# A fused RWKV layer and quantised feed-forward: the first of three matrix powers takes 48 columns instead of 64, and four engines' orders are rewritten

## The reference, cut to what matters

```python
x = x + attn(layernorm(x)) ; x = x + int8_linear(layernorm(x))

# attn: token shift, low-rank mixing into four inputs, then
r, k, v = xrg @ Wr.T, xk @ Wk.T, xv @ Wv.T          # and gates a, ma, mk, decay w, output gate g
kk = normalised per head(k + tanh(xk @ kkk_w1.T) @ kkk_w2);  b = -kk * a
def step(s, (q, w, k, v, a=kk, b)):                  # one token, per head, s is 32x32
    sa = s @ a
    s  = s * w + outer(sa, b) + outer(v, k)
    return s, s @ q
y = groupnorm(y) * ln_w + ln_b + (r*k*faaaa).sum(per head) * v
return (y * g) @ Wo.T

# int8_linear: each row is quantised to int8 by its own maximum, multiplied, scaled, bias added
```

## Time and profile before

| | us |
|---|---|
| median of 3 runs | 3148.51 |
| lowest, highest | 3138.39, 3151.72 |
| the profiled execution's own time | 3128.81 |
| its span, first to last instruction | 3126.8 |

### The profile page before, as it was taken

The page is one execution under the profiler, slowest core; times in us unless marked ns, Lnnn a source line. Parts: engine busy times, 40 slices in busy tenths (PEclk is TensorE's granted clock), DMA queues, the critical chain, the costliest instruction groups (busy, mean ns, idle before and its releaser), DMA issues.

```text
span 3126.8 us, 176469 instructions
## 1 busy us (share of the span) xinstructions
PE 2899.6 (93%) x80128; PEld 2566.1 (82%) x80128; DVE 2496.5 (80%) x4803; ACT 1997.2 (64%) x4486; POOL 1456.9 (47%) x1224
## 2 busy tenths in 40 slices
PE   5999999999999999999999999999999999999995
PEld 5888888888888888888888888888888888888873
DVE  4787887878887888877788788888788887888875
ACT  4666666656666666656666666666666666666663
POOL 5445444445444454444444444544444544544542
PEclk9999999999999999999999999999999999999997
DMA  4122222222222222222222222222222222222211
GB/s 132 41 63 52 47 64 50 47 50 56 56 51 47 64 51 47 64 50 47 50 48 64 51 47 64 51 47 64 51 47 55 60 47 51 56 55 52 63 41 39
DMA packets 92610, 170.74 MB, mean 55 GB/s; under 512 B 13908, under 2 KB 14932, under 8 KB 91864
## 3 DMA queue, kind: packets, MB, share of 16 engines
q1 hardware_dynamic: 91864, 159.45, 21.6%
HBM read 41.97 MB, written 16.78 MB: 19 GB/s over the span
## 4 chain that ended last, share of the span: by engine, by line
PE 86%; issue 5%; DVE 5%; POOL 3%; ACT 1%; DVEq 0%; POOLq 0%; ACTq 0%
PE bank L1228 33%; PE bank_a L1367 12%; PE bank L1429 8%; PE bank_b L1398 4%; PE bank_b L1419 4%; PE bank_b L1345 4%; PE bank_a L1345 4%; PE bank L1235 4%; PE bank_b L1408 3%; PE bank L1310 2%; PE bank L1445 2%; POOL xm_wa L417 1%; PE bank_a L1383 1%; PE bank L1281 1%; PE bank_a L1375 1%
## 5 line engine op out<-in xcount | busy, mean ns | idle before, releaser
L537 ACT ACTIVATE bank<-bank,maa 128x128 f32<-128x128 f32 x1024 | 276.9, 385 | 103.2 <-PE bank L1281 103.2
L1006 DVE STREAM_TRANSPOSE stacked<-bank_b 32x256 f32<-32x256 f32 x512 | 229.2, 448 | 107.7 <-PE bank_b L1419 100.6
L1228 PE MATMUL bank<-xm_rg,w_r 128*128 128x128 f32 x2048 | 280.8, 285 | 7.6 <-issue 6.9
L1228 PE MATMUL bank<-xm_v,w_v 128*128 128x128 f32 x2048 | 281.8, 281 | 2.3 <-issue 2.1
L1429 PE MATMUL bank<-w_o,yc 128*128 128x512 f32 x512 | 259.2, 610 | 12.1 <-DVE yc L826 11.6
L1367 PE MATMUL bank_a<-pw,w_ffn_int 32*32 32x64 f32 x16384 | 258.7, 215 | 3.8 <-DVE pw L826 2.0
L1228 PEld LDWEIGHTS bank<-xm_rg,w_r 128*128 128x128 f32 x2048 | 243.7, 191 | 22.6 <-issue 8.4
L421 POOL TENSOR_TENSOR rs<-rs,minus_half 128x1 f32<-128x1 f32 x64 | 86.6, 1354 | 375.2 <-DVE rs L842 375.2
L1228 PEld LDWEIGHTS bank<-xm_v,w_v 128*128 128x128 f32 x2048 | 253.0, 194 | 8.5 <-issue 2.7
L1367 PEld LDWEIGHTS bank_a<-pw,w_ffn_int 32*32 32x32 f32 x16384 | 236.4, 105 | 23.9 <-issue 13.3
L1228 PEld LDWEIGHTS bank<-xm_k,w_k 128*128 128x128 f32 x2048 | 240.4, 193 | 10.8 <-issue 1.9
(11 more groups left out here) (188 smaller groups left out, 8127.5 us busy)
## 6 DMA issues: line engine op xcount, KB each, us to landing
streamed<-aq_state SPq DMA_DIRECT2D x128, 384.0 KB, 5.2
streamed<-w_ffn_int SPq DMA_DIRECT2D x128, 384.0 KB, 5.3
xin<-in_x SPq DMA_DIRECT2D x128, 128.0 KB, 5.0
xres<-in_x SPq DMA_DIRECT2D x128, 128.0 KB, 2.8
out<-o_sb SPq DMA_DIRECT2D x128, 128.0 KB
w_ffn_int<-in_weight_q SPq DMA_DIRECT2D x1, 2048.0 KB, 10.5
w_k<-in_Wk SPq DMA_DIRECT2D x1, 1024.0 KB
w_r<-in_Wr SPq DMA_DIRECT2D x1, 1024.0 KB
```

The source lines that it names most:

```text
L537: return nc.scalar.activation(out_, in_, func, **kw)
L1006: ins = V.transpose(to[:, :, 1 - c, :], step_part(NEW)[quad(h)])
L1228: ins = mm(bank[:, o * n:(o + 1) * n], weights[:, k, o * P:(o + 1) * P], x[:, k].rearrange("p b t -> p (b t)"), start=(k == 0), stop=(k == ...
```

## The change

The crossing block and the matrix are now neighbours: `first` becomes three sets of G groups with 2 parts each, laid out group by group, where it was six slabs. Set 0 holds the matrix and the crossing block of the tile in work; sets 1 and 2 are the score sets of odd and even tiles for `from_solutions`. The first power multiplies only the 48 columns that are not the identity. The identity's share of the sum, which is the matrix's own right half plus the halves' identity, is formed by two GpSimd sums straight into the right half of `pw`, and `power(m, 1)` on PE waits for them by the new semaphore `g_id`. DVE's sum after the first power then covers 16 columns per group instead of 32. No calls are added or dropped beside the two on POOL; the calls of `tile_step` are in a new order on POOL, ACT, DVE and PE. SP's order stays.

```diff
-        first = sb("first", [P, 6, G, CHUNK])
+        first = sb("first", [P, 3, G, 2, CHUNK])
...
+            def diagonal_sums(m):
+                pool.wait_ge(v_pm, count(m, 1, 1))
+                pool.wait_ge(p_t, count(m, 1, 0))
+                pool.wait_ge(a_tx, count(m, 1, 0))
+                pool.wait_ge(v_t4, count(m, 1, 0))
+                add(pw[:, :, 1, HALF:], first[:, 0, :, 0, 0:HALF], first[:, 0, :, 0, HALF:]).then_inc(g_id, 1)
+
+            def diagonal_ones(m):
+                pool.wait_ge(g_id, count(m, 2, 1))
+                add(pw[:, :, 1, HALF:], pw[:, :, 1, HALF:],
+                    ident_half[:].unsqueeze(1).to_broadcast([P, G, HALF])).then_inc(g_id, 1)
...
             def crossing(m):
                 act.wait_ge(v_pm, count(m, 1, 1))
                 act.wait_ge(v_sums, count(m, POWERS, 0))
-                run(first[:, 1, :, 0:HALF], pairs(bank_a)[:, :, 0, HALF:], ACT.Identity,
+                run(first[:, 0, :, 1, 0:HALF], pairs(bank_a)[:, :, 0, HALF:], ACT.Identity,
...
             def scores_b(m):
                 dve.wait_ge(p_sb, count(m, 1, 1))
-                own = 2 + 2 * (m % 2)
-                tt(first[:, 0:own + 1:own].rearrange("p j g t -> p g j t"), pairs(bank_a), mask_b[:].unsqueeze(1).to_broadcast([P, G, 2, CHUNK]),
+                dve.wait_ge(g_id, count(m, 2, 0))
+                own = 1 + m % 2
+                tt(first[:, 0:own + 1:own, :, 0, :].rearrange("p j g t -> p g j t"), pairs(bank_a), mask_b[:].unsqueeze(1).to_broadcast([P, G, 2, CHUNK]),
...
-                before = first[:, 1] if k == 0 else pw[:, :, 1, :]
-                tt(pw[:, :, 1, :], pairs(bank_a)[:, :, 1, :], before, ALU.add).then_inc(v_sums, 1)
+                if k == 0:
+                    tt(pw[:, :, 1, 0:HALF], pairs(bank_a)[:, :, 1, 0:HALF], first[:, 0, :, 1, 0:HALF],
+                       ALU.add).then_inc(v_sums, 1)
+                else:
+                    tt(pw[:, :, 1, :], pairs(bank_a)[:, :, 1, :], pw[:, :, 1, :], ALU.add).then_inc(v_sums, 1)
...
+                if k == 1:
+                    pe.wait_ge(g_id, count(m, 2, 2))
                 pe.wait_ge(v_ptT, count(m, POWERS + 1, k + 1))
                 for n, g, q in ALL:
-                    ins = mm(bank_a[q, 64 * n:64 * n + 64], pt[q, g, :],
-                             first[q, 0:2, g] if k == 0 else both(pw[q, g]), start=True, stop=True)
+                    if k == 0:
+                        ins = mm(bank_a[q, 64 * n:64 * n + 48], pt[q, g, :], both(first[q, 0, g])[:, 0:48],
+                                 start=True, stop=True)
+                    else:
+                        ins = mm(bank_a[q, 64 * n:64 * n + 64], pt[q, g, :], both(pw[q, g]), start=True, stop=True)
...
                 for j, g, q in step_pairs(c):
                     ins = mm(bank[q, 4 * CHUNK * j + CHUNK:4 * CHUNK * j + 3 * CHUNK], both(u2[q, j]),
-                             first[q, own:own + 2, g], start=False, stop=True,
+                             both(first[q, own, g]), start=False, stop=True,
```

More of the change, by code:

```diff
@@ L196, in rwkv_ffn_kernel @@
         a_pw, a_u, a_y, a_g, a_b2, a_k2, a_vT2 = (sem(f"a_{n}") for n in "pw u y g b2 k2 vT2".split())
-        g_qk, g_qkf, g_rkv, g_aqs = (sem(f"g_{n}") for n in "qk qkf rkv aqs".split())
+        g_qk, g_qkf, g_rkv, g_aqs, g_id = (sem(f"g_{n}") for n in "qk qkf rkv aqs id".split())
         a_e, a_tx, a_xm = sem("a_e"), sem("a_tx"), sem("a_xm")
@@ L494, in tile_step @@
                     norm_rstd(j)
+                if solve:
+                    bonus(m)
+                    diagonal_sums(m)
+                    diagonal_ones(m)
+                    weighted_bonus(m)
                 if project:
-                    kept_keys(i)
                     keys_undecayed(i)
@@ L500, in tile_step @@
                 if project:
+                    kept_keys(i)
+                    keys_weighted(i)
                     removals_undecayed(i)
-                    keys_weighted(i)
-                if solve:
-                    weighted_bonus(m)
                 if finish:
@@ L737, in tile_step @@
                     keys(i)
+                if solve:
+                    key_pairs(m)
+                if finish:
+                    solution(n, 1)
+                if project:
                     ma_gate(i)
                     a_gate(i)
-                if finish:
-                    solution(n, 1)
                 if solve:
+                    value_pairs(m)
                     crossing(m)
-                    key_pairs(m)
                 if project:
@@ L1104, in tile_step @@
                     update_state(n, 1)
-                if mix:
-                    norm_moments(j)
-                if project:
-                    removal_keys(i)
                 if solve:
                     removals_turned(m)
+                    bonus_rows(m)
+                if project:
+                    decay_sums(i)
                 if finish:
                     heads_turned(n)
-                if mix:
-                    norm_variance(j)
-                if project:
-                    decay_sums(i)
                 if solve:
@@ L1147, in tile_step @@
                     shift_mix(j)
-                if project:
-                    removal_directions(i)
                 if solve:
                     power(m, 2)
-                    bonus_rows(m)
+                if project:
+                    key_norm_spread(i)
+                    removal_directions(i)
+                    removals_decayed(i)
                 if finish:
```

104 lines of the change are left out of this document (49 added, 55 removed).

## The result

The changed kernel takes **3169.91 us** (median of 6 runs, 3161.45 to 3181.53) against 3144.18 us for the kernel before (6 runs, 3128.29 to 3151.72). The ratio is 1.010, 95% interval 1.007 to 1.013 (the two medians alone give 1.008): slower by about 1%, where 3120 us was forecast. The profiled execution took 3165.46 us.

The account below looks back on a forecast made before the run. PE was taken to set the pace, with waits for POOL and for late code. Minus 25.6, plus 9 and minus 12 made minus 28.6 us, 0.91% off 3148.5: 3120 us, 8-in-10 range 3092 to 3148.

Parts of the forecast that it names:

- The first power: PE's first power with 48 instead of 64 columns: 0.40 us less per tile, minus 25.6 us, bounds 0 and minus 45.
- The flat price of the first rival: First power: 48 columns cost about what 64 do, saving some 8 us in all; part of a rival with chance 0.22.
- Late code: Holes without a semaphore at the first power take back part of its gain: plus 9 us, bounds 0 and plus 12.
- the 35 us that I had named as a sign of being wrong: Holes at the first power of more than 35 us would show the prediction wrong.
- The wait for `xm_wa`: PE's wait for POOL at `hidden` gets shorter by 0.35 us in 35 tiles: minus 12 us, bounds 0 and minus 38.
- The wait for `g_id` and the two sums: At PE's second power: POOL's two sums end about 4 us before PE asks, so no cost.
- ACT's value copies ahead of `crossing`: ACT before the first power: four value copies, 2.66 us, stay hidden with 0.2 to 0.7 us to spare; zero.
- My slower side: Rival, chance 0.08: ACT's value copies end after PE is ready for the first power; 3184 us.
- `xn` ahead of the affine pieces: ACT before the output projection: spare time falls from 0.88 to 0.16 us; zero, upper bound plus 19 us.
- the term that I put at zero for everything else that moved: Other moved calls, on engines with idle time, end over half a us ahead of their readers; no cost.
- The clock: PE's mean clock was 0.968; a mean off by over 0.01 from that would show the prediction wrong.
- The rival of the eaten gain: Chance 0.22: 48 columns cost about what 64 do or late code takes the gain, and `xm_wa` is no sooner; 3141 us.

Follow-up runs that it names:

- pool_back: The changed kernel with GpSimd's kept_keys and keys_weighted back in their old places: 3099.21 us, ratio 0.9885 to the kernel before.
- act_back: The changed kernel with only ACT's normalised(j) back ahead of power(m, 1): 3122.02 us, ratio 0.996 to the kernel before.
- columns_only: The kernel before with the 48 columns, the new layout and the two sums, all its orders kept: 3132.43 us, ratio 0.9985.
- pool_back_64: The changed kernel with GpSimd's kept_keys and keys_weighted in their old places and 64 columns in the first power: 3107.13 us, ratio 0.9882.
- pool_back_32: The changed kernel, GpSimd's kept_keys and keys_weighted in old places, 32 columns in the first power, crossing-block product left out: 3112.76 us, ratio 0.9882.

## Why the prediction was wrong

*The first power, minus 25.6:* right. The batch is busy 1.56 us; in all 107.8 us against 133.8, minus 26.0. The flat price of the first rival doesn't hold for this packing: 1.56 us lies between the 1.29 us with 32 columns and the 1.99 with 64.

*Late code, plus 9:* near in size at its place (25.9 to 37.2 us, plus 11.3, and past the 35 us that I had named as a sign of being wrong), too small as a whole. All of PE's waits without a semaphore went from 128.0 to 160.0 us, plus 32, where my bound was 12. `solve_step` (L1428) gained 13.6 us of them and `inverse` (L1403) 4.1, which I had not asked about. The hole that the earlier trace rows show behind 122 records is there again, in the same place, with 48 columns:

```profile
1521.48 1.54 PE L1385 MATMUL bank_a<-first,w_ffn_int 32*32 32x48 f32 x122
1525.27 0.28 PE L1385 MATMUL bank_a<-first,w_ffn_int 32*32 32x48 f32 x6 [2.25 <-issue]
```

*The wait for `xm_wa`, minus 12:* right, 38.0 to 25.2 us, minus 12.8.

*The wait for `g_id` and the two sums, 0:* right. They take 0.73 us each, and PE never waits for them; the old code without them is no faster.

*ACT's value copies ahead of `crossing`, 0:* right. PE waits 0.6 us for `first` in the whole run. My slower side was this one, and it didn't happen.

*`xn` ahead of the affine pieces, 0 with 0.16 us to spare:* right by itself. In a tile of `pool_back` the gate product ends at 1548.59 and `project_out` starts at 1548.78, 0.19 to spare. But `act_back` shows what giving up 0.7 us of room meant: it bounds what any later delay may be, and I went on to price the others as if the room were still there.

*The step that failed* is the term that I put at zero for everything else that moved, in the sentence that "all else that moved (`bonus_rows`, `decay_sums`, `kept_keys`, `finish_rows`) lies on engines with idle time and ends ahead of its reader by over half a us". DVE never waited for `kept`, so its reader did have it in time. What it delayed is an operation of another engine that neither reads it nor is read by it: the gate product, 1.71 us instead of 0.69, and with it `project_out`. An idle engine isn't free to be used where its work shuts out a busy one. The price, from `after` to `pool_back`: 1.010 to 0.9885, some 68 us, of which PE's wait at `project_out` shows 47. Of the rest, `low_rank` shows some: its products are busy 76.0 us in the kernel after, where the mix ends 0.06 us ahead of the batch in one tile, and 68.7 in `pool_back`. The remainder is not traced.

*The clock:* 0.978 on the profiled run is 0.010 above 0.968, at the edge of the 0.01 that I had named and on the good side; over all timed runs it is 0.976. By the estimate above the loss would have been larger without it.

*The rival of the eaten gain* (0.22) names what the columns did do: it is `columns_only`'s result, 3132 us, which I had at 3141. In the profiled executions the holes took nearly all of it (25.4 of 27.5 us), at more places than the one I had priced.

Left open: what the holes are, why those at L1428 grew in the new order, and what makes the clock's slow stretches fewer in it.

## What to carry to other kernels

Before moving an elementwise operation of GpSimd, lay its new interval beside VectorE's timeline: if a product or sum with two SBUF inputs begins within it, that one ends nearly its own length after GpSimd's has ended (0.55 us for a length of 0.69), and the question is who reads it and with how much to spare. Spare time ahead of a reader is one account for all edits: when one edit takes 0.7 of 0.9 us, price the others against the 0.2 that is left. A shorter batch on the bounding engine is a gain only as far as the stalls of the whole engine, measured with that edit alone, haven't grown by as much.

## What the hardware showed beyond that

- VectorE's blocked operations in these kernels all read two SBUF operands: the products `yc<-yc,gate` and `xx<-xT` (0.69 and 0.65 to 1.7 us), `vT<-v_sum` (0.75 to 1.32), the `SCALAR_TENSOR_TENSOR` pieces of the mix (73.0 to 129 us in all). It works both ways: GpSimd's `qkT` product went from 1.27 to 2.09 us and `kkp` from 1.19 to 1.61 with the new order, and no cost of it can be seen: `pool_back` has the same two lengths.
- A batch of 64 packed products of 32x32 (128 records) takes 1.99, 1.56, 1.29 and 1.31 us with 64, 48, 32 and 16 columns; the price falls down to 32 and is the same at 16.
- Stalls without a semaphore come at the same record of the same batch whatever its speed: behind 122 records in the kernel before (2.36 us), after (2.25), `columns_only` (2.79), `pool_back_64` (1.54) and `pool_back_32` (2.54). The queue that loads code moved the same 632 packets in each.
